# Cross-attention and an expert-choice FFN: reciprocals within their group, the last maxima placed apart, a normalise out of place, and products that nobody reads

## The reference

```python
h = layernorm(x)                                  # over the last axis
q, k, v = h @ Wq + bq, ctx @ Wk + bk, ctx @ Wv + bv     # 16 heads of 32
x = x + softmax(where(mask, q k^T * 32**-0.5, min)) v @ Wo + bo

# 4096 tokens, 8 experts, each takes its 512 most probable tokens
xf = layernorm(x).reshape(4096, 512)
route_prob = softmax(xf @ Ws + bs).T              # (8, 4096)
vals, routes = top_k(route_prob, 512)
for e in range(8):
    y = gelu(xf[routes[e]] @ W1[e] + b1[e]) @ W2[e] + b2[e]    # 512 -> 2048 -> 512
    final[routes[e]] += y * vals[e]
return x + final
```

## Time and profile before

| | |
|---|---|
| time, three runs | 1755.02, 1756.51, 1756.75 us; median 1756.51 |
| the profiled execution | 1757.38 us, its span 1755.6 us, mean granted TensorE clock 0.96 |
| busy, share of the span | PE 92%, DVE 64%, ACT 56%, POOL 17% |
| start to first score of group 0 | 0 to 61.8 us |
| attention | 61.8 to 959.6 us |
| last projection, normalise, logits | 959.6 to 978.7 us |
| routing of the first experts | 978.7 to 1018.9 us |
| FFN | 1018.9 us to the end |

### The profile page before, as it was taken

How to read it: one execution, slowest core, us unless ns; L and a number is a source line. 1 busy time by engine, 2 the same in 40 slices (tenths; PEclk the granted TensorE clock), 3 DMA queues, 4 the chain that set the end, 5 groups by cost and what they waited for, 6 DMA issues and landing times.

```text
span 1755.6 us, 22169 instructions
## 1 busy us (share of the span) xinstructions
PE 1612.7 (92%) x7763; PEld 1158.5 (66%) x7763; DVE 1116.2 (64%) x1950; ACT 983.8 (56%) x2115; POOL 291.7 (17%) x381
## 2 busy tenths in 40 slices
PE   6799989899898998998988389999999999999997
PEld 4456556466565565665644178788888888888885
DVE  6576776867858768678664656776454545454543
ACT  3788798797987878879776222323232323232321
POOL 3131130211211303113021010102020201010100
PEclk9889999999999999999989589999999999999999
DMA  6453543643526335354270132433334343424340
GB/s 208 124 162 93 169 133 98 180 145 127 175 62 212 114 124 173 103 161 142 92 225 17 55 123 94 127 108 98 138 104 143 95 151 88 159 84 163 88 128 24
DMA packets 132711, 219.88 MB, mean 125 GB/s; under 512 B 17276, under 2 KB 51216, under 8 KB 132600
## 3 DMA queue, kind: packets, MB, share of 16 engines
q1 hardware_dynamic: 115960, 175.85, 31.7%
q0 software_dynamic: 16640, 42.61, 8.7%
HBM read 159.02 MB, written 58.87 MB: 124 GB/s over the span
## 4 chain that ended last, share of the span: by engine, by line
PE 75%; ACT 11%; DVE 8%; DMA 2%; issue 2%; POOL 0%; SPq 0%; ACTq 0%; DVEq 0%; POOLq 0%
PE ps_gen L704 8%; PE ps_gen L705 8%; PE ps_gen L706 8%; PE ps_gen L1802 7%; PE ps_gen L1804 6%; PE ps_gen L1803 6%; ACT ps_gen L1058 5%; PE ps_att L1660 5%; PE ps_gen L1627 5%; PE ps_gen L1649 4%; ACT p_ring L1070 4%; PE ps_gen L1613 3%; PE ps_gen L1614 2%; PE ps_gen L1615 2%; DVE stat L1158 2%
## 5 line engine op out<-in xcount | busy, mean ns | idle before, releaser
L1244 DVE TENSOR_REDUCE nmax<-ps_gen 128x1 f32<-128x512 f32 x512 | 339.0, 684 | 139.8 <-PE ps_gen L1627 137.6
L1070 ACT ACTIVATE p_ring<-ps_gen,keep_scale 128x512 f32<-128x512 f32 x512 | 335.2, 691 | 79.2 <-PE ps_gen L1649 79.1
L1058 ACT ACTIVATE ps_gen<-ps_gen,nmax 128x512 f32<-128x512 f32 x512 | 342.0, 671 | 58.0 <-DVE nmax L1244 57.4
L1127 ACT ACTIVATE gel<-ps_gen,b_cols 128x512 f32<-128x512 f32 x128 | 88.3, 690 | 451.1 <-PE ps_gen L706 450.9
L1495 DVE TENSOR_TENSOR gel_lo<-gel,gel_hi 128x512 fp32r<-128x512 f32 x126 | 87.2, 692 | 284.0 <-ACT gel_hi L1128 284.0
L1627 PE MATMUL ps_gen<-kst,qst 97*128 97x512 f32 x512 | 212.8, 437 | 12.7 <-ACT ps_gen L1058 12.0
L1649 PE MATMUL ps_gen<-qst,kst 99*128 99x512 f32 x512 | 194.4, 432 | 25.2 <-ACT ps_gen L1058 12.9
L704 PE MATMUL ps_gen<-hT_hi,w_hi 128*128 128x512 f32 x512 | 203.3, 397 | 1.5 <-DVE hT_lo L1488 1.5
L706 PE MATMUL ps_gen<-hT_hi,w_lo 128*128 128x512 f32 x512 | 200.4, 391 | 0.0
L705 PE MATMUL ps_gen<-hT_lo,w_hi 128*128 128x512 f32 x512 | 200.4, 391 | 0.0
L1802 PE MATMUL ps_gen<-w_hi,gel_hi 128*128 128x512 f32 x504 | 198.1, 393 | 0.0
(11 more groups left out here) (196 smaller groups left out, 2638.5 us busy)
## 6 DMA issues: line engine op xcount, KB each, us to landing
w_raw<-in_L_ffn_W SPq DMA_DIRECT2D x128, 512.0 KB, 4.6
kst<-qk_rows SPq DMA_DIRECT2D x96, 256.0 KB, 3.9
qst<-qk_rows SPq DMA_DIRECT2D x96, 256.0 KB, 4.8
x_in<-in_x POOLq DMA_DIRECT2D x60, 256.0 KB, 3.7
qk_rows<-kT_hi SPq DMA_DIRECT2D x32, 256.0 KB, 2.0
qk_rows<-kT_lo SPq DMA_DIRECT2D x32, 256.0 KB, 2.0
qk_rows<-qT_hi SPq DMA_DIRECT2D x32, 256.0 KB, 2.0
qk_rows<-qT_lo SPq DMA_DIRECT2D x32, 256.0 KB, 3.7
```

Of the source, the lines that this page charges most:

```text
L1058: e.activation(psum[:, :], psum[:, :], ACT.Exp, bias=nmax[g % 2][:, c], scale=-1.0, accum_out=den[g % 2][:, c]).then_inc(drained_sem("max" ...
L1070: e.activation(p_ring[n % NP_][:, :], ps("score", g, kt, h)[:, :], ACT.Exp, scale=keep_scale[:, b:b + 1]).then_inc(drained_sem("score", g, ...
L1244: e.tensor_reduce(nmax[g % 2][:, h * TB + t:h * TB + t + 1], ps("max", g, h, t)[:, :], AX.X, ALU.min).then_inc(s_min, 1)
```

## The change

- The transposes of the reciprocals (`rden`) of group 0 no longer stand ahead of its first score, but within the group; for all groups their place goes from 0.51 to 0.56.
- The maxima of the last group (31), and the transpose of their rows, have places of their own: -0.39 to 0.56 of group 30 instead of -0.05 to 0.67, and 0.68 instead of 0.73.
- The other places and the lags are set anew. On ACT and DVE the lags changed are `csplit` 0.01 to 0.04, `osplit` 0 to 0.01, `csplit_lo` 0.02 to 0.03, `recip` -0.01 to -0.03, `rden` 0.03 to 0.01, `divide` 0.02 to 0.01, `x1_norm` 0.02 to 0.04.
- The last two tiles of the last batch are normalised into other tiles (`bo_b`, `hnT`), and wait for those to be free instead of for the store of `x_in`. The store of the rows and the transposes read the new place.
- PE gets 8 x 4 + 12 + 12 + 12 = 68 matmuls of 512 columns whose product is never read: four after each count from the third to the tenth, twelve after the ranks, twelve after the list, and two, two, two and six after the four transposes of rows.

```diff
@@ attention_agenda @@
     a.add("recip", 0)
-    a.with_bank("rden", 0)
...
-    K_AT = ((-0.03, 0.38), (0.04, 0.22), (0.06, 0.16), (0.07, 0.07))
-    Q_AT = ((0.41, 0.43), (0.20, 0.28), (0.14, 0.33), (0.20, 0.30))
-    MAX_AT = ((-0.12, 0.59), (-0.07, 0.66), (-0.05, 0.67), (-0.17, 0.59))
-    ROWS_AT = 0.73
-    RECIP_AT, RDEN_AT, OSPLIT_AT = 0.01, 0.51, 0.18
-    V_NEXT_AT = (0.32, 1.29)
-    LOAD_C_AT, SPLIT_C_AT = (-0.13, 0.20), (0.28, 0.48)
-    LOAD_X_AT, STATS_X_AT = (0.21, 0.40), (0.61, 0.96)
-    NORM_X_AT, TURN_X_AT = (0.68, 1.07), (0.97, 1.16)
-    HALF_AT, HALF_FOR = (("residual", 0.02), ("add_bias", 0.33), ("outa", 0.50)), 0.76
-    LATE_AT = (("out", 0.20), ("x1_norm", 0.44), ("route", 0.56), ("logits", 0.66), ("back", 0.74))
+    K_AT = ((0.01, 0.35), (-0.13, 0.22), (0.05, 0.15), (0.05, 0.10))
+    Q_AT = ((0.40, 0.42), (0.21, 0.30), (0.14, 0.34), (0.17, 0.32))
+    MAX_AT = ((-0.11, 0.59), (-0.07, 0.66), (-0.05, 0.67), (-0.17, 0.60))
+    ROWS_AT = 0.70
+    RECIP_AT, RDEN_AT, OSPLIT_AT = 0.03, 0.56, 0.18
+    V_NEXT_AT = (0.32, 1.32)
+    LOAD_C_AT, SPLIT_C_AT = (-0.26, 0.33), (0.29, 0.48)
+    LOAD_X_AT, STATS_X_AT = (0.28, 0.41), (0.66, 0.95)
+    NORM_X_AT, TURN_X_AT = (0.71, 1.05), (0.93, 1.16)
+    HALF_AT, HALF_FOR = (("residual", 0.03), ("add_bias", 0.35), ("outa", 0.49)), 0.76
+    LATE_AT = (("out", 0.20), ("x1_norm", 0.44), ("route", 0.56), ("logits", 0.66), ("back", 0.73))
...
     a.lags = {
-        "sync": {"mask_row": 0.04, "keep_hi": -0.04, "keep_lo": 0.03, "stack_hi": 0.08, "stack_lo": 0.17, "out": 0.03, "x1_norm": 0.07, "back": 0.32},
-        "pool": {"load": 0.06, "residual": -0.08, "rows_lo": -0.02, "recip": -0.01, "stats": 0.07, "out": 0.12,
-                 "add_bias": 0.10},
+        "sync": {"mask_row": 0.05, "keep_hi": -0.02, "keep_lo": 0.02, "stack_hi": 0.12, "stack_lo": 0.21, "out": 0.03, "x1_norm": 0.10, "back": 0.58},
+        "pool": {"load": 0.04, "residual": -0.05, "rows_lo": -0.03, "recip": 0.11, "stats": 0.00, "out": 0.07,
+                 "add_bias": 0.25},
...
+    END_MAX_AT, END_ROWS_AT = (-0.39, 0.56), 0.68
...
         if i + 1 < NG:
-            place(i, MAX_AT[r], [(a.max_of, i + 1, h, t) for h in range(HG) for t in range(TB)])
-            place(i, (ROWS_AT, ROWS_AT), [(a.max_rows, i + 1)])
+            place(i, MAX_AT[r] if i + 2 < NG else END_MAX_AT, [(a.max_of, i + 1, h, t) for h in range(HG) for t in range(TB)])
+            rows_at = ROWS_AT if i + 2 < NG else END_ROWS_AT
+            place(i, (rows_at, rows_at), [(a.max_rows, i + 1)])
             place(i + 1, (RECIP_AT, RECIP_AT), [(a.add, "recip", i + 1)])
-            place(i + 1, (RDEN_AT, RDEN_AT), [(a.with_bank, "rden", i + 1)])
+        place(i, (RDEN_AT, RDEN_AT), [(a.with_bank, "rden", i)])
@@ attention_moe_kernel @@
+        def hn_tile(b, t):
+
+            if (b, t) == (B - 1, TB - 2):
+                return bo_b[:, :]
+            if (b, t) == (B - 1, TB - 1):
+                return hnT[:, :, :].rearrange("p c t -> p (c t)")
+            return x_in[residual_slot(b, t)][:, :]
+
+        def in_place(b, t):
+            return b < B - 1 or t < TB - 2
...
@@ vector_program, x1_norm @@
-                    on.wait_ge(s_x1_store[xs], 16 * agenda.residual_no[b, t])
-                    normalise(("x1", b, t), x_in[xs][:, :], s_norm_x1)
+                    if in_place(b, t):
+                        on.wait_ge(s_x1_store[xs], 16 * agenda.residual_no[b, t])
+                    else:
+                        on.wait_ge(*full("back", b - 1, TB - 1))
+                        on.wait_ge(s_x1, NT)
+                    normalise(("x1", b, t), x_in[xs][:, :], s_norm_x1, hn_tile(b, t))
...
@@ tensor_program @@
+            def keep_busy(n, psum=ps_gen[2]):
+
+                on.wait_ge(s_drained[2], agenda.bank_uses[2])
+                on.wait_ge(s_split_act, 1)
+                for _ in range(n):
+                    e.matmul(psum[:, :], lhsT=w1s[0][0][:, 0, 0:P], rhs=w1s[0][0][:, 0:2, :], start=True, stop=True)
...
             for k in range(len(SHIFTS[FIRST])):
                 count(FIRST, k)
+                if k > 1:
+                    keep_busy(4)
             total(FIRST)
             rank_all(FIRST)
+            keep_busy(12)
             list_slots((0,))
+            keep_busy(12)
...
             for tt in range(TT):
                 turn_rows(0, tt)
+                keep_busy(2 if tt < TT - 1 else 6, ps_up[1])
             up(0)
```

More of the change, by code:

```diff
@@ L302, in attention_agenda @@
-        "pool": {"load": 0.06, "residual": -0.08, "rows_lo": -0.02, "recip": -0.01, "stats": 0.07, "out": 0.12,
-                 "add_bias": 0.10},
-        "act": {"turn": 0.00, "csplit": 0.01, "proj": 0.00, "rows": -0.09, "sum": 0.00, "score": 0.00, "osplit": 0.00,
+        "sync": {"mask_row": 0.05, "keep_hi": -0.02, "keep_lo": 0.02, "stack_hi": 0.12, "stack_lo": 0.21, "out": 0.03, "x1_norm": 0.10, "back": 0.58},
+        "pool": {"load": 0.04, "residual": -0.05, "rows_lo": -0.03, "recip": 0.11, "stats": 0.00, "out": 0.07,
+                 "add_bias": 0.25},
@@ L305, in attention_agenda @@
+        "act": {"turn": 0.00, "csplit": 0.04, "proj": 0.00, "rows": -0.09, "sum": 0.00, "score": 0.00, "osplit": 0.01,
                 "logits": 0.00, "back": 0.00},
-        "dve": {"stats": 0.00, "norm": 0.03, "turn_lo": 0.00, "csplit_lo": 0.02, "proj_lo": 0.00, "max": 0.00, "rows_lo": -0.10,
-                "recip": -0.01, "rden": 0.03, "divide": 0.02, "v": 0.09, "route": -0.01, "osplit_lo": 0.00, "outa": 0.04,
-                "out": 0.00, "x1_norm": 0.02, "back": 0.00},
+        "dve": {"stats": 0.00, "norm": 0.03, "turn_lo": 0.00, "csplit_lo": 0.03, "proj_lo": 0.00, "max": 0.00, "rows_lo": -0.10,
+                "recip": -0.03, "rden": 0.01, "divide": 0.01, "v": 0.09, "route": -0.01, "osplit_lo": 0.00, "outa": 0.04,
+                "out": 0.00, "x1_norm": 0.04, "back": 0.00},
@@ L820, in sync_program @@
                     on.wait_ge(s_norm_x1, n + 1)
-                    e.dma_start(hn_rows[n * P:(n + 1) * P, 0:D], x_in[xs][:, :]).then_inc(s_hn_store[xs], 16)
+                    e.dma_start(hn_rows[n * P:(n + 1) * P, 0:D], hn_tile(b, t)).then_inc(s_hn_store[xs], 16)
                 elif kind == "back" and at[1] == TB - 1:
@@ L1162, in statistics, with normalise @@
                 e.tensor_scalar(rstd[i][:, :], mv[i][:, 1:2], EPS, None, ALU.add).then_inc(s_ln, 1)
-            def normalise(key, tile, done):
+            def normalise(key, tile, done, dst=None):
                 turn, i = agenda.ln_turn[key], stat_slot(key)
                 on.wait_ge(s_rstd, turn + 1)
-                e.tensor_scalar(tile, tile, mv[i][:, 0:1], rstd[i][:, 0:1], ALU.subtract, ALU.mult).then_inc(done, 1)
+                e.tensor_scalar(tile if dst is None else dst, tile, mv[i][:, 0:1], rstd[i][:, 0:1], ALU.subtract, ALU.mult).then_inc(done, 1)
             for kind, *at in agenda.order_of(agenda.lags["dve"]):
@@ L1683, in tensor_program @@
                     b, t = at
-                    xs = residual_slot(b, t)
+                    tile = hn_tile(b, t)
                     on.wait_ge(*free("route", b, t))
@@ L1687, in tensor_program @@
                     for c in range(DC):
-                        last = e.transpose(ps("route", b, t)[:, c * P:(c + 1) * P], x_in[xs][:, c * P:(c + 1) * P], ident[:, :])
+                        last = e.transpose(ps("route", b, t)[:, c * P:(c + 1) * P], tile[:, c * P:(c + 1) * P], ident[:, :])
                     last.then_inc(full_sem("route", b, t), 1)
```

## The result

The changed kernel takes 1738.89 us (median of four runs, 1737.57 to 1742.76); the kernel before, run beside it, 1756.63 (four runs, 1755.02 to 1758.47). The ratio is 0.9902 [0.9883, 0.9922], so it is faster by 17.2 us, give or take 3.5.

What follows compares the result with a forecast made beforehand. PE was taken to bound the kernel almost everywhere, ACT to lead second groups, neither to bind groups 29 and 30. Terms -0.2 - 1.0 - 4.0 - 0.5 - 3.45 = -9.15 gave 1748 us, range 1740 to 1757.

Steps and rivals of the forecast that it cites:

- Places and lags: Attention, all groups: the new places and lags give -1.0 us, between bounds of +5.5 and -8.5.
- The k chunk: Second group of a batch: 0.69 us of PE work crosses into the first group, which PE fills; +5.5 if nothing comes back.
- `rden` one slot later for all groups: Groups other than 0: the reciprocals' transposes move from slot 10 to 11, division nine slots behind; priced at 0.
- places do more: Rival: in second groups a pair of PE's waits for ACT vanishes, -14.8 us, giving 1732.6; chance 0.06.
- the bank of k: Slower rival: second groups keep k's bank longer, one more pair of waits in seven batches, +14.8 us, so 1762; chance 0.08.
- `add_bias` behind `rows_lo`: POOL's order turns round and DVE waits 1.6 us; costs 0, covered by DVE's slack at the end of r = 2, else 12.8.
- Maxima of group 31: End of group 29: early maxima fill ACT's idle time, -4.0 us; PE waits 0.6 us for the stack; bounds -6.5 and +1.
- Unread products: Search, list, rows' transposes and `up(0)`: products bring PE's full clock, -3.45 us; bounds -5 and +2.8.
- clock not held: Rival: in the search the products come too thinly and delay counts, +2.8 us instead of -3.45, so 1753.6; chance 0.13.
- Reciprocals of group 0: First score of group 0: PE's 3.77 us stall is taken over by the rows' DMA; -0.2 us, bounds 0 and 0.4.
- Normalise: Last batch's end: the last normalise begins 0.6 us earlier, not held by the store; -0.5 us, bounds 0 and -0.6.
- Groups 20 and 21 within 0.5 us of their 58.0 together: Sign in the attention that the forecast is right: these two groups together keep their length to within 0.5 us.

Runs made afterwards that it cites:

- e5: Kernel before with only the reciprocals' transposes moved: group 0's into the group, all from 0.51 to 0.56; 1750.74 us, ratio 0.9968.
- e4: Kernel before with only k of a batch's second group spread over -0.13 to 0.22 instead of 0.04 to 0.22; 1751.41 us, ratio 0.9966.
- e3: Kernel before with all other places, lags and the reciprocals' move, without group 31's own places, unread products or the new normalise; 1748.63 us, ratio 0.9948.
- e9: Changed kernel with the maxima and rows of group 31 placed as those of the other groups; 1741.75 us, ratio 0.9921 to the kernel before.
- e2: Kernel before with only the own places of group 31's maxima and their rows; 1753.54 us, ratio 0.9976.
- e1: Kernel before with only the 68 unread products added; 1751.54 us, ratio 0.9962.
- e7: Kernel before with SP holding the first weight loads until the maxima's rows of group 30 have landed; 1752.30 us, ratio 0.9972.
- e8: Changed kernel with eight unread products per round instead of four; 1747.32 us, ratio 0.9933 to the kernel before.
- e11: Changed kernel with first weight loads held for group 30's rows, group 31's first maximum at -0.30, products from the second round; 1737.47 us, ratio 0.9895.

## Why the prediction was right and where it was wrong

**Places and lags: the step that failed.** The term was -1.0, "near the middle, since ACT's 25.64 of 28.2 us leave the second group little to give". Alone the places gave -9.1 by time (from -11.9 to -6.5), around my far end of -8.5; by the ten profiles above it is -7.2 up to group 28. With that, what the stages show adds up: 7.2 for the places, 4.9 for the early maxima, 4.5 for the products, 0.6 for the normalise and 0.2 for the reciprocals of group 0 are 17.4, where the forecast had 1.0, 4.0, 3.45, 0.5 and 0.2. That it comes so near the measured 17.2 is luck, as these are differences of single profiles or of a few, but the places are clearly the term that was off, by 6 of the missing 8 us. The mechanisms were priced wrongly at three points.

- *The k chunk.* I moved 0.69 us of PE's work and asked whether the second group, led by ACT, would give any of it back. It gives back 1.0 in an undisturbed batch. ACT's share of a group is no proof that PE's work there is free: PE works in a fixed order and both engines wait for each other at single places. The rows I had already showed it: in 28.2 us ACT had 2.6 to spare and PE 4.6, so neither engine filled the group. The net is only -0.3 in an undisturbed batch.
- *`rden` one slot later for all groups.* I wrote "For all other groups they move by one slot (10 to 11)" and priced it at 0. It is -0.6 in every undisturbed third group, shown by e5 and by the two timelines: the transposes stood ahead of a maximum that waited for its bank. I had looked at the division behind the transposes and not at what stands next to them in PE's order.
- *Places with a low clock.* In batch 0 the moved work also changes how long the clock is low: in e4 alone the clock is most of group 1's 2.7 us. I had no term for it. e3 gains 3.2 us in batch 0 and 3.8 in batch 7, of its profile's 12.4 us of attention; the other 5.5 are the six batches between, at 0.9 each, as the two points above give. But of these only the steady part and some of batch 0 (2.2 us on average over the six profiles) are shown to belong to the places. The 3.8 of batch 7 aren't: e9 has the same places and none of them, with a granted clock of 0.78 in group 30 where e3 has 0.92.

In the changed kernel the same places gave less in batch 0 (2.0 of 3.2), where its clock was low for longer, group 1 taking 25.9 us against 25.1 in e3. Why it was low for longer I can't say: up to there the two kernels differ in nothing.

**The rival "places do more"** had the right sign and about the right part of the kernel, at 0.06, but the wrong mechanism. It said that a pair of PE's waits for ACT in r = 1 would vanish. Both are still there in batch 6: the profile gives 1.2 us at the maxima and two of 1.9 together at the scores, against 1.2 and 0.9 in batch 3 before. The slower rival, the bank of k, foretold one more such pair; one more wait of 1.0 did appear, and the group got shorter all the same. `add_bias` behind `rows_lo` cost nothing either, though DVE's wait was longer than the 1.6 us that I had worked out. In batch 6:

```profile
822.95 0.69 DVE L1320 TENSOR_TENSOR x_in<-ps_gen,x_in 128x512 f32<-128x512 f32 x1 [3.00 <-POOL x_in L932]
```

Still PE is busy for all of the 27.69 us of the fourth group behind it, as it was for all of 27.78 before. So the cover that I had counted on, DVE's slack, held.

**Maxima of group 31: -4.0.** About right in size: -4.2 in e2, by time and in batch 7 of its profile, and 4.9 by profile in the changed kernel. The way there was different, so the size was in part luck. The stack was not there after 0.6 us but after 2.48, since its DMA took 4.5 us instead of the 3.8 of the earlier trace rows and PE came to it 2.3 us behind the issue. So ACT idles for 2.4 us, and I had filled all of it. What made up for it was my bound "if PE also keeps its clock in group 30": 0.81 became 0.91, and the group is 19.6 us long where I had said 23. ACT's busy run from 905 to 920, which I named as a sign, has the two gaps shown above.

**Unread products: -3.45.** The trace gives -4.5: -2.1 up to `up(0)` and -2.4 in it (I had -2.3). The counts and the search gave -1.2 instead of -0.45 (-0.8 in e1's profile; 0.17 of the 1.2 are in the first round, ahead of any product). I took 0.42 for a warm count from a wider one of a later stage, and it takes 0.37, in six rounds and not five. The rows' transposes and what follows gave -0.66 for -0.45, the list -0.16 for -0.25. By time e1 gives -6.7 (from -9.0 to -4.4), its own profile -4.0, so the smaller number is the safer. The rival "clock not held" is refuted: the granted clock is 1.00 from the fifth round to `up(0)`.

**Reciprocals of group 0: -0.2.** -0.24, as worked out: the transposes' wait of 3.77 turned into the score's wait of 4.26 for the DMA. The score of group 0 itself stands 0.6 us later than before, for reasons ahead of it.

**Normalise: -0.5.** The last one begins without a wait for a store:

```profile
960.85 0.54 DVE L1179 TENSOR_SCALAR bo_b<-x_in,mv,rstd 128x512 f32<-128x512 f32 x1
...
961.83 0.55 DVE L1179 TENSOR_SCALAR hnT<-x_in,mv,rstd 128x512 f32<-128x512 f32 x1 [0.44 <-POOL rstd L858]
```

Its 1.04 us are 0.44 now, and it waits for its power: 0.6, as said. From the last division to `ind` the changed kernel takes 20.2 us, as before, but PE's clock was low for 2.2 us at the end of its group 31 and for 8.0 us in this stretch (6.8 before). Two kernels with the old normalise had the same low stretches, e1 (2.3 and 8.0) and e7 (2.0 and 8.2), and took 20.8; that is 0.6 more. In e8 to e11, where group 31 had the full clock, the stretch takes 19.1 to 19.6, and in those with the old normalise and the full clock 19.7 to 20.3. So the 0.6 is borne out, but no run changes the normalise alone.

**The signs I named.** "Groups 20 and 21 within 0.5 us of their 58.0 together" came true (58.0), and was a bad sign: the pair holds no third group, and group 21 was one of the disturbed ones. One whole undisturbed batch on each side would have been the right thing to compare.

**What stays open.** The times of single parts (-4.2 to -9.1) are each good to 2 or 3 us only, and some are larger than their profiles explain. e5 has -5.6 by time and 3.6 us less attention in its profile, of which batches 1 to 6 gave only 1.7 and batch 7 the rest, though the third groups alone would give 3.6 if all were undisturbed. And which spacing of work keeps the clock up in groups 1 and 29 to 31 was not worked out: the runs show that it moves, and that it also differs between kernels with the same instructions, not by what rule.

## What to carry to other kernels

When a planner's places move, compare whole periods in which nothing disturbs the kernel, group by group, and read the order of the instructions next to the one that moved: here the price of a step was the wait of its neighbour. If no engine fills a stretch, taking work out of it can shorten it by all of that work and more, however busy the second engine looks. And one profile of a place with a low clock proves little: the same places gave 3.8 us in batch 7 of e3 and nothing in e9. Unread products held the clock through a search that is mostly waiting and paid from the first warm rounds on; their number must fit the idle time of a round (four fit by 0.67 us, eight didn't and took 3.6 us more from the first `ind` to `up(0)`).
